# Two program blocks made one: the QKV stage joined to the rest, and the write weights prepared in small pieces

## The reference

```python
qkv_in = rat_read(hidden_states, attn_read_w, attn_read_g, attn_read_b, 3)
attn_out = attention(qkv_in, qkv_w, position_ids)
hidden_states = rat_write(hidden_states, attn_out, attn_wod_w, attn_wab_w, attn_wab_b, attn_du_w, attn_du_b)
mlp_in = rat_read(hidden_states, mlp_read_w, mlp_read_g, mlp_read_b, 2)
...
scores = jnp.where(mask, scores, jnp.float32(-1e+30))
p = jax.nn.softmax(scores, axis=-1)
o = jnp.einsum('bhqk,bkhd->bqhd', p, v)
```

## Time and profile before

| | us |
|---|---|
| three runs | 2353.85, 2365.98, 2349.78; median 2353.85 |
| profiled execution | 2358.97, span 2357.4 |
| mean granted TensorE clock | 0.966 of 2.4 GHz |
| TensorE matmuls busy | 2194.2 (93% of the span) |
| VectorE busy | 1335.8 (57%) |
| ScalarE busy | 1065.8 (45%) |
| GpSimd busy | 986.0 (42%) |
| QKV stage | to about 330 |
| first scores of attention | 342.04 |

### The profile page before, as it was taken

How to read it: one execution, slowest core, us unless ns; L and a number is a source line. 1 busy time by engine, 2 the same in 40 slices (tenths; PEclk the granted TensorE clock), 3 DMA queues, 4 the chain that set the end, 5 groups by cost and what they waited for, 6 DMA issues and landing times.

```text
span 2357.4 us, 34030 instructions
## 1 busy us (share of the span) xinstructions
PE 2194.2 (93%) x11560; PEld 1796.0 (76%) x11560; DVE 1335.8 (57%) x1745; ACT 1065.8 (45%) x1594; POOL 986.0 (42%) x613
## 2 busy tenths in 40 slices
PE   6889857999997999799999999998799999999999
PEld 4777745666666888688788899997588887888887
DVE  6778746777765898423332266777365364265222
ACT  2444425888885787621321356665322222122111
POOL 0111114999997877300000288784053153153110
PEclk9999976999998999899999999999899999999999
DMA  5687742333324766445554568788565565465442
GB/s 179 217 254 238 234 141 58 97 103 95 103 69 132 264 231 225 171 123 173 151 166 125 193 244 309 286 294 304 176 197 187 158 202 175 152 199 184 154 141 98
DMA packets 208916, 424.60 MB, mean 180 GB/s; under 512 B 16482, under 2 KB 132194, under 8 KB 181940
## 3 DMA queue, kind: packets, MB, share of 16 engines
q1 hardware_dynamic: 208820, 423.31, 55.4%
HBM read 284.31 MB, written 138.67 MB: 179 GB/s over the span
## 4 chain that ended last, share of the span: by engine, by line
PE 62%; DMA 8%; DVE 6%; ACT 4%; issue 3%; POOL 2%; SPq 1%; DVEq 0%; ACTq 0%; POOLq 0%
PE s_psF L2628 7%; PE s_m_psG L2254 7%; PE s_psF L2629 7%; PE s_psF L2630 7%; PE s_m_psU L2254 7%; PE s_psO L871 4%; PE s_w_psA L1838 4%; PE s_w_psB L1838 4%; PE s_psS L819 4%; DMA s_f_q<-wq 3%; PE s_psX L848 3%; DMA y<-s_f_xb 2%; DVE s_a_mx L897 2%; PE s_w_psT L1870 1%; DVE s_w_ab L1613 1%
## 5 line engine op out<-in xcount | busy, mean ns | idle before, releaser
L2628 PE MATMUL s_psF<-s_f_wh,s_f_xh 128*128 128x512 f32 x1024 | 402.5, 393 | 12.6 <-DVE s_f_xl L2507 8.1
L2630 PE MATMUL s_psF<-s_f_wh,s_f_xl 128*128 128x512 f32 x1024 | 400.9, 391 | 0.0
L991 POOL TENSOR_TENSOR s_a_pl<-s_a_pf,s_a_ph 128x1024 fp32r<-128x1024 f32 x128 | 301.9, 2394 | 21.2 <-ACT s_a_pf L954 21.1
L2503 ACT ACTIVATE s_f_xh<-s_f_xl 128x2048 fp32r<-128x2048 f32 x64 | 122.7, 1917 | 388.8 <-PE s_psF L2630 310.7
L897 DVE TENSOR_REDUCE s_a_mx<-s_psS 128x1 f32<-128x512 f32 (+7 forms) x256 | 185.1, 754 | 108.4 <-PE s_psS L827 107.9
L2601 POOL TENSOR_TENSOR s_f_xb<-s_f_xb,s_f_fb 128x512 f32<-128x512 f32 x64 | 95.2, 1487 | 358.6 <-DMA s_f_xb<-x 340.1
L2628 PEld LDWEIGHTS s_psF<-s_f_wh,s_f_xh 128*128 128x128 f32 x1024 | 194.1, 190 | 57.1 <-DVE s_f_xl L2507 10.9
L2006 POOL TENSOR_TENSOR s_w_yl<-s_w_y,s_w_yh 128x1024 fp32r<-128x1024 f32 x32 | 76.0, 2396 | 372.5 <-ACT s_w_yh L1918 372.5
L2630 PEld LDWEIGHTS s_psF<-s_f_wh,s_f_xl 128*128 128x128 f32 x1024 | 193.9, 189 | 40.7
L2507 DVE TENSOR_TENSOR s_f_xl<-s_f_xl,s_f_xh 128x2048 fp32r<-128x2048 f32 x64 | 161.2, 2518 | 82.3 <-ACT s_f_xh L2503 82.3
L2629 PE MATMUL s_psF<-s_f_wl,s_f_xh 128*128 128x512 f32 x512 | 201.4, 393 | 0.0
(11 more groups left out here) (310 smaller groups left out, 5599.5 us busy)
## 6 DMA issues: line engine op xcount, KB each, us to landing
s_f_xl<-xnT SPq DMA_DIRECT2D x64, 1024.0 KB, 5.8
s_q_xt<-xT SPq DMA_DIRECT2D x16, 1024.0 KB, 7.7
s_q_xc<-xP SPq DMA_DIRECT2D x16, 1024.0 KB, 9.8
hsD<-s_q_hs SPq DMA_DIRECT2D x16, 1024.0 KB, 4.9
s_w_hin<-hsD SPq DMA_DIRECT2D x16, 1024.0 KB, 5.1
hs<-s_w_res SPq DMA_DIRECT2D x16, 1024.0 KB, 3.9
s_m_raw<-giT SPq DMA_DIRECT2D x32, 512.0 KB, 4.7
mlpT<-s_m_mo SPq DMA_DIRECT2D x64, 256.0 KB, 2.5
```

The lines of the kernel that those rows point to most:

```text
L991: pool.tensor_tensor(pl[:, r, cols], pf[:, j - 1], ph[:, r, cols], ALU.subtract).then_inc(pl_ok, 1)
L2628: pe.matmul(out[:], xh[:, u % 2, kt], high(c, kt), start=(kt == 0), stop=False)
L2630: mm = pe.matmul(out[:], xl[u % 3][:, kt], high(c, kt), start=False, stop=(kt == KD - 1))
```

## The change

1. The QKV stage is no longer a block of its own. Its five engine parts are functions that `build_rest` calls first in its one block. `retire` is gone, and so are the two meetings of all engines. The QKV buffers get fixed places in the memory map of the rest.
2. In the drain of the QKV stage, SyncE loads heads 0 and 1 behind slot 17, once the stores of the first 14 tiles have landed. GpSimd sets the rows of ones behind slot 16. TensorE, ScalarE and VectorE go on to attention without a meeting; TensorE waits for what the banks need.
3. The write weights are prepared one 128x632 block a slot. SyncE issues the small loads and the first block at the end of its slot 2, and at the end of slots 3 to 6 the next, each after the low part of the block before is done, as there is now one raw buffer. ScalarE copies block i at the head of slot i+3. VectorE makes the constants and block 0 in slot 3, `w_spf` and block 1 in slot 4, blocks 2 and 3 in slots 5 and 6 and the bias row in slot 7, all ahead of the maxima of that slot.
4. The semaphores of QKV and attention are reused by the second write as well. GpSimd clears them in the MLP, and SyncE's first load of the second write waits for that (`cleared`).

```diff
-        def prepare_scalar(act):
-            for i in range(parts):
-                ...
-                act.activation(wh[:, part], wraw[:, part], ACT.Copy).then_inc(w_hi, 1)
+        def prepare_sync(sp, slot):
+            i = slot - AT
+            if i == 0:
+                sp.dma_start(rw[:], io["wr2"]).then_inc(rw_in, 16)
+                ...
+            if 0 <= i <= KH:
+                if i:
+                    sp.wait_ge(w_lo, i)
+                sp.dma_start(wraw[:], io["wo1"][:, i] if i < KH else io["bsm1"]).then_inc(w_in, 16)
+
+        def prepare_scalar(act, slot):
+            i = slot - AT - 1
+            if 0 <= i < KH:
+                act.wait_ge(w_in, 16 * (i + 1))
+                act.activation(wh[:, i], wraw[:], ACT.Copy).then_inc(w_hi, 1)
...
+        def prepare_vector(dve, slot):
+            i = slot - AT - 1
+            if i == 0:
+                constants(dve)
+            if i == 1:
+                ...
+                dve.tensor_tensor(spf[:, HD:].rearrange("p (t j) -> p t j", j=HD), ...)
+            if 0 <= i < KH:
                 dve.wait_ge(w_hi, i + 1)
-                dve.tensor_tensor(wl[:, part], wraw[:, part], wh[:, part], ALU.subtract).then_inc(w_lo, 1)
+                dve.tensor_tensor(wl[:, i], wraw[:], wh[:, i], ALU.subtract).then_inc(w_lo, 1)
+            if i == KH:
+                ...
+                dve.tensor_copy(brow[:], wraw[:]).then_inc(prep, 1)
+                dve.wait_ge(prep, 4)
+                dve.tensor_tensor(brow[64:P, :], wraw[64:P, :], brow[64:P, :], ALU.subtract).then_inc(ready, 1)
```

```diff
+        def sync_ahead(sp, i):
+            if i == 1:
+                qkv["rows_read"](sp)
+                qkv["stored"](sp, TILES - 2)
+                load(sp, Step(None, 0, HEADS), 0)
+                load(sp, Step(None, 1, HEADS), 1)
+            if i == 3:
+                qkv["projected"](sp)
...
-            steps(sp, HEADS, LAST + 1, RING, body, LAST + 2, after=after)
+                if s.reg is None:
+                    late(s.off)
+            steps(sp, HEADS, LAST + 1, RING, body, LAST + 2, start=2, after=after)
...
+        def gpsimd_ahead(pool, i):
+            if i == 0:
+                qkv["rows_read"](pool)
+                qkv["added"](pool, TILES - 1)
+                pool.memset(ka[K3:KM_, :, :].bitcast(F32), 1.0).then_inc(ones_ok, 1)
+                ...
```

```diff
         @block.sync
         def _(sp):
-            def early(slot):
-                if slot == 1:
-                    w1["prepare_sync"](sp)
-
-            att["sync"](sp, early, lambda i: w1["sync_ahead"](sp, i))
+            qkv["sync"](sp, lambda i: att["sync_ahead"](sp, i))
+            att["sync"](sp, lambda slot: w1["prepare_sync"](sp, slot), lambda i: w1["sync_ahead"](sp, i))
...
         @block.gpsimd
         def _(pool):
+            qkv["gpsimd"](pool, lambda i: att["gpsimd_ahead"](pool, i))
             att["gpsimd"](pool)
             w1["gpsimd"](pool, lambda i: mlp["gpsimd_ahead"](pool, i))
             pool.wait_ge(mlp["mm_u"], KS)
             for handle in renewed:
                 pool.sem_clear(handle)
+            pool.sem_inc(cleared, 1)
...
-            build_qkv(nc, io, k)
-        retire(nc, k["settled"])
         build_rest(nc, io, k, zone)
```

More of the change, by code:

```diff
@@ L117 @@
 TAKEN = []
[L120 to L130, removed]
 def allocators(nc, ctx, tag=""):
@@ L375, in at_slot @@
             return s.reg is None and s.off == n
+        sb = shelf(nc, "s1_", zone["tables"], zone["tables"] + 4 * zone["slot"])
         xt = sb("q_xt", [P, 2, KD, P])
         xc = sb("q_xc", [P, 2, D])
[L379 to L397, removed]
+        hs = more("q_hs", [P, D])
+        sh = more("q_sh", [P, 2])
+        yr = more("q_yr", [P, KD, OW])
+        yn = more("q_yn", [P, O, H])
+        yth = more("q_yth", [P, O, KH, P], F32R)
+        ytl = more("q_ytl", [P, O, KH, P], F32R)
+        bst = more("q_bst", [P, 4, 6])
+        bsy = more("q_bsy", [P, O, 6])
+        mv = more("q_mv", [P, O, 2])
+        sx = more("q_sx", [P, 2, 5])
+        sy = more("q_sy", [P, 5, O])
+        more = shelf(nc, "s1_", zone["raw"], zone["stage"])
+        ra = more("q_ra", [P, 2 * H])
+        rb = more("q_rb", [P, 2 * H])
+        qk = more("q_qk", [P, 2 * H])
+        qth = more("q_qth", [P, 2, KH, P], F32R)
+        qtl = more("q_qtl", [P, 2, KH, P], F32R)
+        sb = shelf(nc, "s1_", zone["raw"], zone["end"])
+        wraw = sb("q_wraw", [P, KH, O * H])
         X_AGG, X_EPS, X_NEG, X_INV = 5, 6, 7, 8
@@ new lines, in rows_read, with stored, state_stored, projected @@
+        def rows_read(sp):
+            sp.wait_ge(y_mm, 4 * TILES)
+            sp.wait_ge(hs_ok, TILES)
+            sp.wait_ge(x_norm, 8 * TILES)
+        def stored(sp, tiles):
+            sp.wait_ge(qk_out, 16 * 4 * tiles)
+        def state_stored(sp):
+            sp.wait_ge(hs_out, 16 * TILES)
+        def projected(eng):
+            eng.wait_ge(qkv_mm, 3 * TILES)
+        def reads_out(pe):
+            pe.wait_ge(y_norm, 11 * (TILES - 1) + Y_LESS)
+        def banks_out(pe):
+            pe.wait_ge(qt_lo, 2 * TILES)
+            pe.wait_ge(rot_ab, 2 * TILES)
+            pe.wait_ge(v_ok, TILES)
@@ L1048, in build_write1 @@
         m32 = sb("w_m32", [P, HD])
-        sb = shelf(nc, "s3_", zone["tables"] + 4 * zone["slot"], zone["tables"] + 6 * zone["slot"])
-        wraw = sb("w_raw", [P, KH, NW])
-        braw = sb("w_braw", [P, NW])
         flat64 = sb("w_flat", [P, P])
+        wraw = shelf(nc, "s3_", zone["stage"], zone["end"])("w_raw", [P, NW])
         sb = shelf(nc, "s3_", zone["XB"], zone["XA"])
@@ L1073, in build_write1 @@
         psL = psT[1][0:S0, 0:P]
-        PT = 2
-        parts = KH // PT
-        w_in = [sem(f"w_in{i}") for i in range(parts)]
+        w_in = sem("w_in")
         rw_in, small_in = sem("rw_in"), sem("small_in")
@@ L1749, in sync_ahead @@
             if i == 0:
+                sp.wait_ge(cleared, 1)
                 sp.wait_ge(mlp["x_lo"], 2 * TILES)
```

653 lines of the change are left out of this document (322 added, 331 removed).

## The result

| | before | after |
|---|---|---|
| median of 8 runs each | 2358.35 | 2377.61 |
| lowest to highest | 2347.74 to 2368.15 | 2370.30 to 2382.36 |
| ratio, 95% interval | | 1.0082 [1.0050, 1.0113] |
| profiled execution, span | 2358.97, 2357.4 | 2374.69, 2372.6 |
| mean granted clock there | 0.966 | 0.958 |

The changed kernel is slower by 19.3 us, 0.8%, and no run of it was faster than the slowest of before. The forecast was +4.8 us on 2353.85, that is 2358.65; its range ended at 2370. Of the 19.0 us between it and 2377.61, 4.5 lie in the starting point (2353.85 was the median of three runs, 2358.35 is that of eight) and 14.5 in the effect.

The account below looks back on a forecast made before the run. TensorE, busy 93% of the span, was taken as the bound, leaving its idle time and clock. Terms -16.3 - 3.3 + 16.2 + 8.2 = +4.8 us on 2353.85 gave 2359, range 2341 to 2370.

Parts of the forecast that it names:

- clock term: Attention slots 3 to 7: one 3.5 us stretch at 1.2 GHz after each of five waits, 5 x 1.65 = 8.2 us.
- gap: Between QKV and attention: TensorE idles 19.38 us; removing the meetings and clearing was to gain 16.3 us.
- Part 1: QKV to attention: first reduction starts at 327.45 instead of 343.75, a gain of 16.3 us.
- Part 2: Attention's slot 1 without the weight preparation: reduction starts at 356.98 instead of 360.31, a gain of 3.3 us.
- Part 3: Preparation in slots 3 to 7: ScalarE's copy and the VectorE-GpSimd lock delay the maxima, costing 16.2 us together.
- the double: Slots 3 to 7: upper bound of the clock's cost, two low-clock stretches after each wait instead of one.
- forecast case: Whole kernel: lock holds and one low-clock stretch follows each wait, +4.8 us; said to span 2352 to 2367; chance 0.55.
- the lock's share: Slots 3 to 7: VectorE and GpSimd wait for each other's whole instruction; waits 16.2 us with it, 8.0 without.
- no lock: Rival, slots 3 to 7: no VectorE-GpSimd lock or kindly falling borders, cost 8.0, net -5.0, 2349; chance 0.22.
- Hidden: Rival, slots 3 to 7: preparation hidden within the slots, only some 2 us added, net -17.6, 2336; chance 0.08.
- The clock did come back between the waits: Answers a rival: clock stays at 1.2 GHz through slots 4 to 6, +26.5 on top of +4.8, 2385; chance 0.07.
- The loads were in time: Answers a rival: first heads load too late, only about 3.5 of 16.3 us saved, net +17.6, 2371; chance 0.05.

Follow-up runs that it names:

- the last version: Changed kernel, one piece a slot behind group 2's maxima, SyncE loading raw blocks a slot after the buffer is freed: 2338.26 us, ratio 0.9924 to before.

## Why the prediction was wrong

The mechanisms of attention were right. Two steps failed. The clock term was too small, 8.2 us forecast and 11.8 measured, and everything behind attention's slot 7 was put at nothing and came to 7.8. The gap brought 2.4 us less than forecast and the waits cost 1.4 more. These four make up the 15.2 us between +4.8 and +20.0.

Against the means of the five traces each, which differ by 20.0 us (the medians by 19.3):

| term | forecast | measured |
|---|---|---|
| gap | -16.3 | -13.9 |
| slot 1 | -3.3 | -3.3 |
| slots 3 to 7, waits of TensorE | +16.2 | +17.6 |
| slots 3 to 7, clock | +8.2 | +11.8 |
| rest of attention | 0 | +1.2 |
| write 1 | 0 | +10.4 |
| after write 1 | 0 | -3.8 |

The waits are TensorE's idle time in these slots, 18.4 us against 0.9 before, and the clock is the growth of its busy time over the same 328 matmuls, 64.7 against 52.9. Measured they add to -13.9 - 3.3 + 29.4 + 1.2 + 10.4 - 3.8 = +20.0.

- **Part 1** was right in its mechanism. 327.45 was forecast for the first reduction, and the changed kernel's five traces have it at 324.85 to 331.44, 327.57 in the mean; that the mean is so close is partly luck, with such a spread. The start of the subtraction was off: the traced execution of the kernel before had reached this place 2.3 us later than the mean of five (356.7 against 354.4), and that part of the gain was not there to have. A single trace carries such an error in every landmark.
- **Part 2** was right: slot 1 shrank from 17.2 to 13.9 us.
- **Part 3, the waits**, came out at 2.50, 3.37, 4.72, 4.74 and 3.06 in slots 3 to 7, against 3.2, 4.0, 2.8, 2.8 and 3.4. Slots 5 and 6 carry the error. I had read GpSimd's borders off an undisturbed slot. A slot that starts late shifts them, and in slot 5 the border that VectorE was to meet had passed 0.04 us before. That the sum is off by only 1.4 us is partly luck: three slots were forecast too long by 0.3 to 0.7 and two too short by 1.9.
- **The clock** is the step that failed most within attention: one stretch of 3.5 us at the low clock for each wait was charged, "5 x 1.65". The trace shows four of 6.8 us in slots 4 to 7. Behind slot 3's wait there was none of its own, but the low stretch that attention begins with went on for 9.05 us of this slot, against 1.5 before (4.2 to 9.1 against 0.7 to 2.7 over the five traces). Part of each stretch fell into the wait itself, so the term is 11.8 and not the double, 16.4. I had priced it from a wait of at most 1.6 us, and these waits were up to three times as long. The double was among my bounds.
- **Write 1** had no term at all. The sum took everything behind attention as unchanged, since its code is. Half of the missing time came from there: +10.4, or +7.8 together with what lies around it. The windows show where it went, a lower clock over the same matmuls; why it is lower there is not shown, so this part of the cause stays open.
- **Slips in the working**: for SyncE's head load, 5.1 + 2.7 + 3.6 is 11.4 and not 11.7, which changes nothing. The 2352 to 2367 given for the forecast case do not follow from its words: half to one and a half of the clock term and half to all of the lock's share (16.2 less 8.0) give about 2350 to 2363, and 2367 is the clock term doubled. The start of slot 8, forecast at about 445, came at 448.54.

The rivals: no lock is refuted by 0.80 against 2.97 us for one subtraction, and by 0.35 against 2.00 for one copy. Hidden is refuted for this order of the pieces, and the last version shows that another order has it. The clock did come back between the waits (0.66 to 1.00 in any 10 us of it). The loads were in time. Even the clock term doubled (16.4) gives only 16.2 + 16.4 - 19.6 = +13.0; the range lacked a term for stages whose code stays the same.

## What to carry to other kernels

Work moved into slots whose engines have slack costs little for its length (here a piece of 0.8 to 1.2 us in a slot of 10.7 was free, and one of 1.3 to 1.8 at the head of the slot cost up to 0.5), and much for its waits: on an engine whose own work of the slot stands first, on a port that another engine holds, and on a queue that must load the next tile. Give each moved piece a producer one slot back and a consumer one slot on, one piece a slot, and look for the place where its engine idles. Half a percent in a kernel bound by TensorE needs several traces of each kernel, since stages whose code did not change moved by more than the forecast.

## What the runs showed that was not expected

- One 128x632 subtraction of two SBUF inputs on VectorE took 0.80 with GpSimd idle, 1.28 to 1.83 at the head of a slot beside it, 2.97 where it just missed GpSimd's border and 4.33 at the longest, but only 0.81 to 1.17 behind group 2's maxima, the first between GpSimd's small piece and its next group.
- A wait of 1.17 us of TensorE in attention left the clock up; those of 3.37, 4.72, 4.74 and 3.06 each had 6.8 us at 1.2 GHz around their end.
- Write 1's 1346 matmuls took 204.9 to 227.7 us over all traces, at a mean clock of 0.97 in the shortest.
